# Output steps of a transformer kernel's tail in two row tiles, gate products over two pairs of PSUM banks

## The reference

```python
x = x + a_alpha * attention(ada_rmsnorm(x, t, ...), W_q, W_k, W_v, W_o)     # 16 heads of 16
g = ada_rmsnorm(x, t, ffn_gamma_w, ffn_beta_w)
x = x + f_alpha * ((silu(g @ gate_w.T) * (g @ hidden_w.T)) @ out_w.T + out_b)   # hidden width 1024
x = layernorm(x) * weight + bias + tanh(t @ lin_w.T + lin_b)
x = x * weight + bias
```

## Time and profile before

| | |
|---|---|
| median of 3 runs | 753.93 us (753.05 to 753.97) |
| the profiled execution, its own time | 755.2 us |
| its span in the trace | 753.4 us |
| mean granted TensorE clock | 0.988 |
| TensorE busy (matmul) | 712.2 us, 95% |
| VectorE busy | 532.9 us, 71% |
| ScalarE busy | 467.1 us, 62% |
| POOL busy | 391.6 us, 52% |

### The profile page before, as it was taken

How to read it: one execution, slowest core, us unless ns; L and a number is a source line. 1 busy time by engine, 2 the same in 40 slices (tenths; PEclk the granted TensorE clock), 3 DMA queues, 4 the chain that set the end, 5 groups by cost and what they waited for, 6 DMA issues and landing times.

```text
span 753.4 us, 17410 instructions
## 1 busy us (share of the span) xinstructions
PE 712.2 (95%) x6660; PEld 501.2 (67%) x6660; DVE 532.9 (71%) x797; ACT 467.1 (62%) x860; POOL 391.6 (52%) x493
## 2 busy tenths in 40 slices
PE   6698999899999999999999999999999999999995
PEld 5343444467777677767677667767777667679895
DVE  4787787777677767777677767777677766336765
ACT  4467777775667657675666666775666655753431
POOL 4365143552378625865367533866257544872533
PEclk9889999999999999999999999999999999999998
DMA  7677557456434635274453654264354620331210
GB/s 228 169 236 247 194 172 266 121 165 207 151 96 144 191 133 170 63 228 140 143 151 107 207 155 155 60 192 162 99 171 127 178 81 3 90 92 64 54 48 29
DMA packets 63275, 107.17 MB, mean 142 GB/s; under 512 B 10480, under 2 KB 18344, under 8 KB 63192
## 3 DMA queue, kind: packets, MB, share of 16 engines
q1 hardware_dynamic: 61892, 104.66, 45.6%
q10 hardware_dynamic: 1172, 1.20, 0.6%
q0 software_dynamic: 128, 0.20, 0.1%
HBM read 57.50 MB, written 37.52 MB: 126 GB/s over the span
## 4 chain that ended last, share of the span: by engine, by line
PE 66%; DMA 8%; DVE 7%; issue 6%; POOL 5%; ACT 5%; SPq 2%; ACTq 0%; POOLq 0%; DVEq 0%
PE ps_x L1483 15%; PE ps_o L1459 12%; PE ps_j L1354 10%; PE ps_o L1496 9%; PE ps_s L1443 7%; PE ps_m L1424 6%; DVE mx L1174 3%; ACT prob L967 2%; DMA d_c<-reciprocal_scratch 2%; DMA reciprocal_scratch<-d_s 2%; DMA out_scratch<-o_raw 1%; DMA stack_scratch<-qk_hi 1%; PE ps_m L1483 1%; PE ps_s L1483 1%; DMA n_x<-n 1%
## 5 line engine op out<-in xcount | busy, mean ns | idle before, releaser
L1174 DVE TENSOR_REDUCE mx<-ps_m 128x2 f32<-128x1024 f32 x211 | 256.8, 1217 | 49.1 <-PE ps_m L1424 48.8
L967 ACT ACTIVATE prob<-ps_s 128x1024 f32<-128x1024 f32 x219 | 223.6, 1021 | 45.8 <-PE ps_s L1443 44.1
L1459 PE MATMUL ps_o<-prob,v 128*32 128x512 f32 x1024 | 127.5, 600 | 0.1
L1443 PE MATMUL ps_s<-qs,ks 64*128 64x512 f32 x438 | 101.3, 457 | 7.8 <-issue 4.0
L674 POOL TENSOR_TENSOR a_lo<-act_y,a_hi 128x256 fp32r<-128x256 f32 x100 | 73.6, 736 | 62.1 <-ACT a_hi L1000 62.0
L1424 PE MATMUL ps_m<-ks,qs 64*128 64x512 f32 x422 | 90.7, 424 | 9.2 <-DVE mx L1174 5.5
L1483 PE MATMUL ps_x<-n_x,gh_hi 64*128 64x256 f32 x872 | 97.2, 280 | 0.7 <-DMA n_x<-n 0.7
L1215 DVE SCALAR_TENSOR_TENSOR act_y<-act_y,ps_x 128x256 f32<-128x256 f32 x109 | 45.8, 420 | 73.1 <-ACT act_y L993 73.1
L1483 PE MATMUL ps_x<-n,gh_hi 64*128 64x256 f32 x872 | 97.0, 280 | 0.0
L1443 PEld LDWEIGHTS ps_s<-qs,ks 64*128 64x128 f32 x438 | 41.6, 184 | 76.7 <-issue 50.5
L1483 PEld LDWEIGHTS ps_x<-n,gh_hi 64*128 64x128 f32 x872 | 76.0, 186 | 2.6 <-issue 0.2
(11 more groups left out here) (182 smaller groups left out, 1476.3 us busy)
## 6 DMA issues: line engine op xcount, KB each, us to landing
qs<-stack_scratch SPq DMA_DIRECT2D x30, 512.0 KB, 4.7
ks<-stack_scratch SPq DMA_DIRECT2D x30, 512.0 KB, 6.3
stack_scratch<-qk_hi SPq DMA_DIRECT2D x56, 256.0 KB, 3.6
out_scratch<-o_raw SPq DMA_DIRECT2D x32, 256.0 KB, 2.3
n_x<-n SPq DMA_DIRECT2D x32, 256.0 KB, 3.7
stack_scratch<-qk_lo SPq DMA_DIRECT2D x28, 256.0 KB, 3.9
on_lo<-out_scratch SPq DMA_DIRECT2D x16, 256.0 KB
d_c<-reciprocal_scratch SPq DMA_DIRECT2D x16, 256.0 KB
```

Source lines behind the costliest of these rows:

```text
L967: act.activation(prob[:, n % 3, 2 * h:2 * h + 2, :], score_pair(n, h)[:], ACT.Exp, scale=SCALE).then_inc(p_r, 1)
L1174: dve.tensor_reduce(mx[:, group % 2, :, h, qt], max_pair(mp)[:], AX.X, ALU.max).then_inc(mx_red, 1)
L1443: mm = pe.matmul(score_pair(n, j)[:, s, :], ks[r:r + 64, g, j, kb * P:(kb + 1) * P], qs[r:r + 64, g, j, :], start=True, stop=True)
L1459: mm = pe.matmul(ps_o[32 * i:32 * i + 32, :], v[:, at:at + 32], prob[:, n % 3, i, :], start=(kb == 0), stop=(kb == TT - 1), skip_group_che ...
```

## The change

In the tail, an output step becomes 12 matmuls of 64 rows: each of the six is split over array rows 0 to 63 and 64 to 127, one half summed in the first bank of ps_s and the other in the second. VectorE adds the two sums: instead of one product it does a copy of the first from PSUM to sc, an addition of the second, and the product with tab_f, each waiting for the one before. The next half's first output step waits for the addition (f_sum_r) and no more for the product (sc_r). The first output step of the tail waits for the last exponentials (p_r) and no more for the copy o_raw of ps_o. Gate products lose ps_s and rotate over ps_m and ps_x, so that gate(e) waits for y_r of the second step before it. Chunks of the middle go on with ps_o.

```diff
@@ -286,7 +286,7 @@
         def gh_banks(e):
 
-            return ps_x if e < TAIL else (ps_m, ps_x, ps_s)[(e - TAIL) % 3]
+            return ps_x if e < TAIL else (ps_m, ps_x)[(e - TAIL) % 2]
...
@@ -1183,8 +1183,17 @@
                     dve.wait_ge(f_done, end)
                     dve.wait_ge(tab_f_in, 16 * ((end - 1) // (2 * JC) + 1))
-                    dve.tensor_tensor(sc[:], ps_f, tab_f[:].unsqueeze(1).broadcast_to([P, 2, D]),
-                                      ALU.mult).then_inc(sc_r, 1)
+                    factor = tab_f[:].unsqueeze(1).broadcast_to([P, 2, D])
+                    if what[0] == "F":
+                        dve.tensor_tensor(sc[:], ps_f, factor, ALU.mult).then_inc(sc_r, 1)
+                    else:
+                        top, bottom = (ps_s[:, r].rearrange("p (t n) -> p t n", t=2) for r in range(2))
+                        halves = what[1] - CHUNKS * CH // JC
+                        dve.tensor_copy(sc[:], top).then_inc(f_sum_r, 1)
+                        dve.wait_ge(f_sum_r, 2 * halves + 1)
+                        dve.tensor_tensor(sc[:], bottom, sc[:], ALU.add).then_inc(f_sum_r, 1)
+                        dve.wait_ge(f_sum_r, 2 * halves + 2)
+                        dve.tensor_tensor(sc[:], sc[:], factor, ALU.mult).then_inc(sc_r, 1)
...
@@ -1484,13 +1493,17 @@
-            def project_out(e, out, first, end):
-
-                j = e % JC
+            def a_made(e):
+
                 if e < TAIL:
                     pe.wait_ge(a_lo_r, e + 1)
                 else:
                     pe.wait_ge(a_tail_r, e - TAIL + 1)
+
+            def project_out(e, out, first, end):
+
+                j = e % JC
+                a_made(e)
...
@@ -1508,10 +1521,18 @@
                 hf, j = e // JC, e % JC
                 if j == 0:
                     if CH * CHUNKS == e:
-                        pe.wait_ge(o_r, NG * B)
+                        pe.wait_ge(p_r, 2 * NU)
                     else:
-                        pe.wait_ge(sc_r, SC_NO["H", hf - 1])
-                project_out(e, ps_f, j == 0, j == JC - 1)
+                        pe.wait_ge(f_sum_r, 2 * (hf - CHUNKS * CH // JC))
+                a_made(e)
+                for t in range(2):
+                    for m, (a, c) in enumerate(PARTS):
+                        for r in range(2):
+                            rows = slice(64 * r, 64 * r + 64)
+                            mm = pe.matmul(ps_s[:, r, D * t:D * t + D], A[a][rows, e % RING, t * P:(t + 1) * P],
+                                           OW[c][rows, j, :], start=(j == 0 and m == 0 and t == 0),
+                                           stop=(j == JC - 1 and m == 2), skip_group_check=True)
+                mm.then_inc(f_done, 1)
```

More of the change, by code:

```diff
@@ L225, in build @@
         gh_full = sem("gh_full"); t_r = sem("t_r"); s_r = sem("s_r"); y_r = sem("y_r")
-        a_hi_r = sem("a_hi_r"); a_lo_r = sem("a_lo_r"); a_tail_r = sem("a_tail_r"); f_done = sem("f_done")
+        a_hi_r = sem("a_hi_r"); a_lo_r = sem("a_lo_r"); a_tail_r = sem("a_tail_r"); f_done = sem("f_done"); f_sum_r = sem("f_sum_r")
         stat_r = sem("stat_r"); mv_r = sem("mv_r"); centre_r = sem("centre_r"); rstd3_r = sem("rstd3_r")
```

## The result

| | before | changed |
|---|---|---|
| median, first session | 754.06 us (11 runs) | 757.83 us (11 runs), ratio 1.0050, 95% interval 1.0035 to 1.0066 |
| median, second session | 754.48 us | 756.74 us (12 runs), ratio 1.0035, interval 1.0018 to 1.0053 |
| span of the profiled execution | 753.4 us | 754.7 us (its own time 756.51 us) |
| granted clock, mean over the executions | 0.9879 (89) | 0.9847 (23) |

The change makes the kernel slower by 2.3 to 3.8 us. The forecast was 756.7 us, +2.8 us, in a range of 753.6 to 758.6.

A forecast was written before the change was run, and what follows sets the result against it. TensorE was taken to bound the tail. Gate 126's balance of -0.36 us plus 1.44 at the end gave +1.1, the clock 1.7: +2.8 on the 753.93 us median, 756.7 us, range 753.6 to 758.6.

The forecast's parts named there:

- the term of 1.7 us for the clock: Granted clock falls once at or just after the WO jobs, following a 2.1 us wait: +1.7 us; chance 0.45.
- (b): At WO, outputs 104 and 105 between the two jobs bring two more changes of shape: +0.4 us.
- (a): 673 to 689.8 us: savings hidden by the chain to on_lo; gain 0, wait before WO grows 0.43 to 2.1 us.
- (c): Half 13's sum: three VectorE operations delay gate 116 by 1.33 us, gate 117 by 0.26 more, 1.6 us in all.
- (d): 718 to 739 us: five groups of outputs (114 to 123) lose both changes of shape, -1.95 us.
- (e): After the last output matmul, the product becomes copy, add, product with nothing beside it: +1.44 us.
- The second loss of clock: Rival: waits at outputs 112 and 113, or 703 to 707 us, cost another 1.7 us, 758.4; chance 0.13 with tiles apart.
- the faster rival: TensorE is waited for throughout, so each removed change of shape gains: -2.9 us, 751.0 us; chance 0.12.

The follow-up runs named there:

- e6: Changed kernel plus 30 unread 16-column matmuls in TensorE's first long wait, to move the instruction fetches; ratio 1.0086 against the kernel before.
- e4: Changed kernel plus 40 unread matmuls on TensorE ahead of the first WO job; ratio 1.0041 against the kernel before.
- e2: Kernel before with copy, addition and product in place of the one product at a half's end; ratio 1.0037, +2.8 us.
- e3: Changed kernel with one product of the first bank in place of the three operations, second bank's sum left out; ratio 1.0009 against the kernel before.
- e10: e7 plus ten unread 16-column matmuls in TensorE's wait at the start, to move the instruction fetch; ratio 1.0031 against the kernel before.
- e0: Changed kernel measured again, unaltered; ratio 1.0035 against the kernel before.
- e5: Changed kernel with the second WO job right behind the first, ahead of outputs 104 and 105; ratio 1.0053 against the kernel before.
- e8: e7 plus half 15 in row tiles except its last four steps, with the second bank's sum done early; ratio 0.9990 against the kernel before.
- e9: e7 plus all of half 15 in row tiles, its sum at the end; ratio 0.9999 against the kernel before.
- e1: Kernel before with tail gate products rotating over two pairs of banks, ps_m and ps_x, nothing else; ratio 1.0012.
- e7: Kernel before with row tiles for half 14 alone (outputs 112 to 119) and two pairs of banks; ratio 0.9971, -2.2 us.
- the two fillings: Changed kernel with 40 or 30 unread matmuls ahead of the first WO job; ratios 1.0041 and 1.0035 against the kernel before.

## Why the prediction was right, and where it was not

The direction and the size hold: slower, 756.7 us against 757.83 and 756.74 us, +2.8 us against +3.8 and +2.3. The agreement of the totals is in part luck: the medians of the two sessions are 1.5 us apart, so they can't tell 2.8 from the 4.1 of the profile, where a term of 1.2 us was missing, and whether the term of 1.7 us for the clock is in them at all was not shown. In the profiles the three stretches are 0, +2.1 and +0.7 us by the forecast's steps (0.4 for WO and 1.7 for the clock; then 0.94 + 0.26 - 1.95 + 1.44) and +1.21, +1.78 and +1.10 us as measured. Places in the tail are taken beside the second transposes FT1 (710.38 us before, 710.53 with the change), so that what lies ahead is left out; the forecast's +1.33 us at gate 116 held the 0.4 us of (b) and is 0.94 us here.

| step | forecast | measured |
|---|---|---|
| (a) wait before WO | 2.1 | 3.15; 2.09 with the fetch moved and the shortest last read (e6) |
| (a) o_raw to WO | 0 | +1.21 |
| (b) two changes of shape at WO | +0.4 | +0.25 (e6), +0.30 (e4) |
| the clock after WO | +1.7 | +1.48 and +1.37 (e4 against the two profiles of the change) |
| FT0 to FT1 | 0 | -0.05 |
| (c) gate 116 | +0.94 | +1.03 |
| (c) gate 117, with two pairs of banks | +1.20 | +1.17 |
| (d) from gate 117 to the last outputs | -1.95 | -1.80 (gate 127) |
| a_low(127) | 0 | +0.30 |
| (e) the sum at the end | +1.44 | +1.46 |
| FT0 to the end | +0.7 | +1.10 |

**What was right.** Row tiling brings no speed of its own: two 64-row matmuls side by side step at 0.12 us, like one of 128 rows. Changes of shape cost 0.2 us each and pay where TensorE is what is waited for. The chain to on_lo swallows what is won before WO. The second loss of clock, a rival, did not come: the waits of 1.14, 0.45 and 1.08 us behind FT0 left the granted clock at 1.00. The Trainium skill (TensorEngine Tiling (Array Packing), section Key Properties), whose rule that a change of tiling mode drains TensorE I had as the faster rival, states no price; the trace agrees that a change costs time, 0.38 us a unit with two of them (4.68 against 4.30), though it does not show the drain itself. It does not decide for the whole, since only the changes behind WO count. The section PSUM Bottleneck of that page of the Trainium skill bears out more fully: the evacuation (e2: +2.58 us) costs more than the tiles bring (e3: -1.71 us from FT0 on).

**What failed.** It is the step in (a) that read "The four transfers on SP's queue and the reciprocal are as before". They are the same transfers in the same order, but the write is 0.85 us longer, because the instruction fetch of TensorE's program meets it. That is most of the difference between the profile's sum, +4.1 us, and the forecast's 2.8, and most of what made the wait 3.15 us instead of 2.1. Of the rest, the last read takes 0.51 us more and the read of d_s 0.18 us less. It also matters for the clock: in e6, where the wait was the 2.09 us that the prediction had, the clock did not fall. The forecast had a fall from a wait of 2.1 us; the one profile of such a wait speaks against it. The four profiles of waits of 2.84 to 3.45 us behind the change all show it. So the term of 1.7 us was right in size, but the forecast had it from a wait that in its one profile brought no fall. With a short write and a last read as long as in e2 the wait would be nearly 3.0 us (2.09 + 4.35 - 3.45, an estimate), so the fetch is not the only thing that can make it long; and e10's 3.01 us brought no fall either.

**A small miss at the end.** VectorE starts a_low(127) 0.63 us earlier beside FT1 (33.66 us behind it against 34.29), but the copy starts only 0.33 us earlier than the product did (35.51 us against 35.84): a_low takes 0.73 us instead of 0.43, which (e) did not look at. The timelines of POOL and VectorE, before:

```profile
743.21 1.34 POOL L755 TENSOR_TENSOR xr<-xr,w 128x512 f32<-128x512 f32 x1
...
744.67 0.43 DVE L1223 TENSOR_TENSOR a_lo<-act_y,a_hi 128x256 fp32r<-128x256 f32 x1 [0.48 <-ACT a_hi L1000]
```

and with the change:

```profile
743.35 1.29 POOL L755 TENSOR_TENSOR xr<-xr,w 128x512 f32<-128x512 f32 x1
```

With the change VectorE is there at 744.19 us, while POOL's multiplication still runs. The other profiles agree: in the eight where the two overlap (changed, e0, e3, e4, e5, e6, e8, e9) a_low(127) takes 0.73 to 0.81 us and ends 0.28 or 0.29 us after POOL's operation; in the five where they don't (before, e1, e2, e7, e10) it takes 0.42 to 0.43 us. It looks as if it gets on only when POOL's operation is over. That is an observation; no run moved POOL's operation by itself.

**What stays open.** How much of the clock's 1.4 us is in the medians (the two fillings say 0.3 us, with over 1 us of uncertainty). What the clock asks for beside a long wait, since it fell in e3 behind 2.84 us and not in e10 behind 3.01. Why the last read of the chain takes 3.45 to 4.36 us: a second fetch on queue 8 falls near its start in the changed kernel, e0, e3, e4 and e5 and near its end in before, e1, e2, e7, e8 and e9, but does not sort the values (3.75 to 4.36 us in the former, 3.51 to 4.35 in the latter). And whether the fetch meets the write in unprofiled executions as well: it is tied to TensorE's place in its program, and the medians of e6 and e10 don't isolate it.

## What to carry to other kernels

A change of tile shape costs TensorE 0.2 us a time, but it is worth taking out only where TensorE is what is waited for, and against it stands what joining the split sum costs the other engine: here the one half whose sum lies beside TensorE's work gains 0.3% (e7, interval 0.05 to 0.53%, one session), while all four together lose 0.4%. When an edit changes the number of instructions, look where the instruction fetches fall against a transfer on the critical path.

## What was not expected of the hardware

- A fetch of 0.02 MB of TensorE's instructions takes 0.9 to 1.5 us of DMA time (1.06 in the changed kernel), and with it a 256 KB write takes 2.8 to 3.2 us instead of 2.0 when it comes 0.8 to 1.4 us after the start of o_raw, and 4.1 us when it comes 1.8 us after it. At 1.1 us before the start, or 2.1 us and more after it, the write takes 1.99 to 2.07 us.
- The granted clock fell behind idle stretches of 2.84 to 3.45 us in four profiles, did not fall after 2.09 us (e6), and did not after 3.01 us (e10) either: the length of the wait alone does not settle it.
- A VectorE subtraction of 256 columns (a_low), 0.42 us alone, takes 0.73 to 0.81 us where it starts beside POOL's multiplication of 512 columns, and ends 0.28 or 0.29 us after that.
